# A test-time-training layer with a mixture of experts on one core: experts on rows sorted by group instead of all experts on all rows

## The chip, the cores and the metric

The kernel runs on one core of one Trainium2 chip. The metric is the device time of one execution in microseconds (us). Engines: TensorE (PE, its weight loads PEld), VectorE (DVE), ScalarE (ACT), GpSimd (POOL), and SyncE (SP), which issues DMAs.

## The reference

Input x is 2048 x 256 in f32. After a layer norm over the 256 columns (xn), the output is x + attention part + expert part.

```python
# attention part, heads of 64, chunks of 128 rows, carried state W0, W1, W2, M0, M1, M2
def step(carry, xi):
    ...
    dw0, dw1, dw2 = gradients from q, k, v of this chunk, plus M * mean(momentum)
    M0n, M1n, M2n = dw0, dw1, dw2
    dw0, dw1, dw2 = newtonschulz5 of each        # five iterations X <- aX + (bA + cAA)X, A = X X^T
    return (renorm(W0 + dw0), renorm(W1 + dw1), renorm(W2 + dw2), M0n, M1n, M2n), out
...
scores over a window of 256 keys, softmax, times v
return (ttt_out + attn_out) @ Wo

# expert part: 32 experts in 4 groups of 8, for each row 2 groups and 8 experts in them
scores = sigmoid(xn @ gate_w.T);  top 2 groups by the sum of their 2 best;  top 8 experts in those
xl = xn @ fc1_w.T                                # 256 -> 128
routed = (sum over chosen e of w_e * relu(xl @ w1[e].T)**2 @ w2[e].T) @ fc2_w.T
shared = relu(xn @ shared_up_w.T)**2 @ shared_down_w.T      # 256 -> 512 -> 256
```

Sixteen chunks of 128 rows follow one another, since each needs the weights that the one before leaves. The expert part has no such dependence.

## The kernel before

Everything is f32, and all loops are unrolled. A start prepares chunk 0, then 16 steps follow (`body(i, last)` on each engine), one a chunk. A step i has a head (`k_side`, `q_side`, `grads`, `sums`, `x_first`: key side, query side, gradients and their norm), then 20 stages of Newton-Schulz: in stage st, `ns_turn` (transpose), `ns_gram`, `ns_square` or `ns_apply` by st % 4 on TensorE, for two pairs of heads (g = 0, 1), with `xt` and `ns_x` on ScalarE and `ns_a` and `ns_m` on VectorE in between. The tail has `update`, `row_pow`, `renorm` and `turn_w`/`w_T` (the new weights and their transposes). Semaphores order the engines; each engine runs its own list in order. A dictionary `fill` says by hand what else an engine does after which stage: the attention of step i, the preparation of chunk i+1, and the experts.

Experts: all 32 are computed on all 128 rows of a chunk, in 8 units of 4 experts. `h_up` multiplies the latent rows `xlT` by four weight tiles into the bank HB, `h_relu` on ScalarE does relu and square into `hq`, `y_down` multiplies back into the bank YB, and `y_acc` on VectorE adds YB, scaled by the row's weight (zero where the expert isn't chosen), to `acc`. `y_first` does that for unit 0 on ScalarE. All expert weights (4 MB) stay in SBUF. `route(m)` on VectorE picks groups and experts for one chunk in 13 short instructions or so, one after each half stage. `shared_up` and `out_down` are the shared expert, whose square runs on GpSimd; `fc1` and `out_fc2` change the width. GpSimd does the powers (`power`), `window` and `prep_kl`. SP loads x twice a chunk and stores the result.

```python
fill = {0: [lambda: ln_norm(m), lambda: att_scale(i)], 2: [lambda: y_acc(i, 1)],
...
for st in range(4 * NI):
    for g in range(G):
        if st % 4 in (1, 2):
            (ns_a, ns_m)[st % 4 - 1](i, g, st // 4)
        if st > 10 and routing:
            routing.pop(0)()
    for f in fill.get(st, []):
        f()
```

## Time and profile before

| | |
|---|---|
| median of 3 runs | 794.46 us (792.43 to 794.57) |
| profiled execution | 793.87 us |
| its span in the trace | 792.1 us |
| busy: TensorE, its weight loads | 745.1 us (94%), 639.6 us (81%) |
| busy: VectorE, ScalarE, GpSimd | 612.0 (77%), 463.0 (58%), 184.5 (23%) |
| DMA read, written | 11.41 MB, 2.10 MB |

The profile gives each engine's busy time; a busy TensorE is not one at its peak. The chain that ended last follows the end of the program back from instruction to instruction through whatever released each. The granted clock (PEclk) is 1.00 at full speed and 0.50 at the lower of TensorE's two levels.

### The profile page before, as it was taken

How to read it: one execution, taken by the hardware profiler on the slowest of the kernel's cores; microseconds unless marked ns; L12 is line 12 of the kernel's file. 1: busy time of each engine (PE TensorE's matmuls, PEld its weight loads, DVE VectorE, ACT ScalarE, POOL GpSimd, SP SyncE). 2: the span in 40 equal slices, each digit the busy share in tenths (PEclk: the TensorE clock that was granted, in tenths of full speed). 3: DMA queues.
4: the chain of work that ended last, by engine and by line, in shares of the span. 5: the costliest groups of instructions: out<-in, count | busy, mean ns of one | idle time of the engine just before them, and what ended most of it. 6: DMA issues, size and time to landing. Idle time of an engine off the chain costs nothing.

```text
span 792.1 us, 24469 instructions
## 1 busy us (share of the span) xinstructions
PE 745.1 (94%) x9776; PEld 639.6 (81%) x9776; DVE 612.0 (77%) x2448; ACT 463.0 (58%) x1146; POOL 184.5 (23%) x257
## 2 busy tenths in 40 slices
PE   4899999999999999999999999999999999999997
PEld 2878788788887878878788787887878888788886
DVE  4768778787887868878688786987869878697765
ACT  2665565655655656555556655566555665655754
POOL 1412223122231222312222122220222203222020
PEclk9899999999999999999999999999999999999999
DMA  8100000000000000000000000000000000000000
GB/s 319 68 8 15 9 3 21 2 14 10 2 22 2 16 8 2 22 2 15 8 3 21 2 15 10 2 22 2 15 8 2 22 2 15 8 2 15 2 15 8
DMA packets 9809, 15.07 MB, mean 19 GB/s; under 512 B 1120, under 2 KB 8928, under 8 KB 9440
## 3 DMA queue, kind: packets, MB, share of 16 engines
q1 hardware_dynamic: 7904, 7.80, 3.3%
q10 hardware_dynamic: 1792, 5.70, 1.8%
q8 instruction: 78, 1.28, 0.7%
q14 instruction: 35, 0.29, 0.1%
HBM read 11.41 MB, written 2.10 MB: 17 GB/s over the span
## 4 chain that ended last, share of the span: by engine, by line
PE 74%; ACT 15%; DVE 6%; issue 4%; DMA 1%; SPq 0%; DVEq 0%
PE M L630 23%; PE CC L630 21%; PE HB L630 14%; PE YB L630 11%; ACT hq L415 6%; DVE acc L1332 3%; ACT L570 2%; ACT XT L415 2%; DVE Am L1144 2%; PE CC L739 1%; DMA rows<-in_rows 1%; ACT sq L415 1%; ACT prT L415 1%; PE CC L701 1%; ACT X L415 1%
## 5 line engine op out<-in xcount | busy, mean ns | idle before, releaser
L630 PE MATMUL YB<-e_s,hq 128*128 128x128 f32 x1024 | 140.8, 280 | 11.1 <-DVE acc L1332 9.4
L1332 DVE SCALAR_TENSOR_TENSOR acc<-YB,cw,acc 128x128 f32<-128x128 f32 x448 | 125.3, 342 | 27.3 <-PE YB L630 27.1
L630 PE MATMUL HB<-xlT,e_s 128*128 128x128 f32 x1024 | 143.1, 283 | 0.4 <-ACT xlT L415 0.4
L300 POOL TENSOR_TENSOR r<-r,half 128x3 f32<-128x3 f32 (+1 forms) x78 | 77.9, 1011 | 267.8 <-DVE r L1021 152.6
L630 PEld LDWEIGHTS YB<-e_s,hq 128*128 128x128 f32 x1024 | 124.2, 191 | 17.4 <-issue 15.3
L415 ACT ACTIVATE hq<-HB 128x512 f32<-128x512 f32 x128 | 76.3, 596 | 101.5 <-PE HB L630 101.5
L630 PEld LDWEIGHTS HB<-xlT,e_s 128*128 128x128 f32 x1024 | 126.8, 193 | 6.8 <-ACT xlT L415 0.7
L415 ACT ACTIVATE hq<-hq 128x512 f32<-128x512 f32 x128 | 80.7, 630 | 4.1
L630 PEld LDWEIGHTS CC<-XT 64*64 64x64 f32 x1800 | 43.2, 133 | 32.7 <-ACT XT L415 30.7
L630 PE MATMUL CC<-XT 64*64 64x64 f32 x1800 | 55.6, 232 | 10.3 <-ACT XT L415 10.3
L415 ACT ACTIVATE XT<-CC 128x256 f32<-128x256 f32 x150 | 48.8, 376 | 26.3 <-PE CC L701 26.2
L1144 DVE TENSOR_TENSOR Am<-CC,shifts 128x192 f32<-128x192 f32 x150 | 48.5, 348 | 20.2 <-PE CC L630 20.2
L630 PE MATMUL M<-wall,xnT 128*128 128x512 f32 (+1 forms) x128 | 57.1, 553 | 4.5 <-DMA rows<-in_rows 4.5
L630 PEld LDWEIGHTS CC<-Am 64*64 64x64 f32 x1800 | 42.5, 133 | 22.4 <-DVE Am L1144 16.9
L630 PEld LDWEIGHTS CC<-X,Mp 64*64 64x64 f32 x1800 | 45.5, 133 | 16.5 <-issue 8.8
L630 PE MATMUL CC<-Am 64*64 64x64 f32 x1800 | 54.9, 230 | 3.5 <-DVE Am L1144 3.5
L630 PE MATMUL CC<-X,Mp 64*64 64x64 f32 x1800 | 56.1, 229 | 0.2
L1150 DVE SCALAR_TENSOR_TENSOR Mp<-CC,rests 128x192 f32<-128x192 f32 x150 | 48.6, 350 | 4.8 <-PE CC L630 4.3
L415 ACT ACTIVATE sig<-M 128x512 f32<-128x512 f32 (+1 forms) x32 | 15.7, 490 | 52.2 <-PE M L630 52.2
L415 ACT ACTIVATE X<-CC 128x192 f32<-128x192 f32 x150 | 43.4, 336 | 4.0
L1021 DVE TENSOR_REDUCE r<-sq 128x8 f32<-128x512 f32 x16 | 11.0, 686 | 44.4 <-ACT sq L415 44.4
L331 POOL COPY akT<-akT 128x256 f32<-128x256 f32 x16 | 6.3, 397 | 157.8 <-issue 157.8
(181 smaller groups left out, 1487.3 us busy)
## 6 DMA issues: line engine op xcount, KB each, us to landing
xa<-in_x SPq DMA_DIRECT2D x16, 128.0 KB, 2.2
e_s<-in_e1T ACTq DMA_DIRECT2D x1, 2048.0 KB, 12.7
e_s<-in_e2T ACTq DMA_DIRECT2D x1, 2048.0 KB, 19.2
xr<-in_x SPq DMA_DIRECT2D x16, 128.0 KB, 2.2
out<-ot SPq DMA_DIRECT2D x16, 128.0 KB, 1.7
wall<-in_wall SPq DMA_DIRECT2D x1, 820.0 KB, 5.9
up_s<-in_upT ACTq DMA_DIRECT2D x1, 512.0 KB, 14.3
down_s<-in_downT ACTq DMA_DIRECT2D x1, 512.0 KB, 20.3
```

What stands on the lines that cost most here:

```text
L300: return pool.tensor_tensor(dst, src, expo[:, 0:n], ALU.pow)
L331: pool.tensor_copy(akT[:, :, 0, :], akT[:, :, 1, :])
L415: return nc.scalar.activation(out_, in_, func, **kw)
L570: act.preload_act_table_set("sigmoid_and_others")
L630: return pe.matmul(out_, lhsT, rhs, start=start, stop=stop)
L701: pe.transpose(CA[g][:, P:2 * P], X[g][:, 1:3, :].rearrange("p w c -> p (w c)"), ident[:, :])\
L739: ins = pe.transpose(CA[g][0:HD, w * P:(w + 1) * P], Wn[g][:, w, :], ident[:, :])
L1021: nc.vector.tensor_reduce(r8[:, 0, :], heads(sq8[:, :], 8), AX_X, ALU.add).then_inc(e_ss8, 1)
L1144: nc.vector.tensor_tensor(Am[g][:, :, :], PROD[g], shifts[:, it, :].unsqueeze(1).to_broadcast([P, 3, HD]), ALU.add)\
L1150: nc.vector.scalar_tensor_tensor(Mp[g][:, :, :], PROD[g], NS[it][2], rests[:, it, :].unsqueeze(1).to_broadcast([P, 3, HD]), ALU.mult, ALU. ...
L1332: ins = nc.vector.scalar_tensor_tensor(acc[:, e, :], y, w, acc[:, e, :], ALU.mult, ALU.add)
```

## The change

Four things change together.

1. **Experts on sorted rows.** Layer norm, gate and fc1 of all 16 chunks are computed in step 0 and at the start of step 1 (`ln_turn`, `gate_pair`), and `route()` runs once for all rows, on VectorE from stage 1 of step 1 into step 2. Each row is written twice, once for each of its two groups, with the 8 weights of that group, to its place in a table in HBM sorted by group (32 indirect DMAs of 128 rows by GpSimd, `scatter`). The table has at most 35 tiles of 128 rows, each with one group. A tile needs only its group's 8 experts, in 2 units of 4. SP fetches for each tile the two weight blocks by a register read from `owner_i`, the rows, and the rows' weights, which it writes to HBM and reads back to all partitions (rings of 3 buffers). `h_weight` on VectorE multiplies a unit's 128x512 squares by those weights, and `y_slot` adds all 8 experts of a tile up in PSUM. The tile's result goes to HBM (`keep`); 32 indirect DMAs (`gather`) bring it back in steps 14 and 15, and `last_sum`, `last_turn`, `last_fc2` and `last_out` finish pairs of chunks.
2. **Units in slots.** Each step but the last has 7 slots (`PER`) for a unit's up half and 7 for a down half, two slots later. Row units fill slots 25 to 94 (`FIRST`, 70 units). The shared expert of each chunk is a unit of its own in the slots of `SHARED`, outside these (steps 1 to 3, 13 and 14): 8 matmuls up, 4 of 256 columns down.
3. **Weights group by group.** `update(i, g)` follows stage 19 of each head pair at once with its row sums, and `renorm` scales all three matrices by one multiply.
4. x stays in SBUF, the layer norm is applied by ScalarE, and `prep_qk` moves from stages 4 and 5 to the head, where `shared_up` was.

```diff
+PER = 7
+FIRST = 3 * PER + 4
+SHARED = [PER + 3, PER + 4, PER + 5, PER + 6, 2 * PER, 2 * PER + 1, 2 * PER + 3, 2 * PER + 4, 2 * PER + 6, 3 * PER, 3 * PER + 1,
+          13 * PER + 5, 13 * PER + 6, 14 * PER, 14 * PER + 1, 14 * PER + 2]
...
+            def load(j):
+                b = j % RING
+                if j >= RING:
+                    sp.wait_ge(e_y, at_slot[FIRST + HALVES * (j - RING + 1) - 1][0] + 1)
...
+                first = sp.value_load(owner_i[0:1, j:j + 1], min_val=0, max_val=E - EPG)
+                sp.dma_start(e1_s[b][:, :, :], e1T[:, bass.ds(first, EPG), :]).then_inc(e_tile[b], 16)
+                sp.dma_start(e2_s[b][:, :, :], e2T[:, bass.ds(first, EPG), :]).then_inc(e_tile[b], 16)
...
+            def spread(j):
+                b, n = j % RING, j // RING
+                sp.wait_ge(e_rows[b], 16 * (n + 1))
+                sp.dma_start(cw_d[j, :].rearrange("(p e) -> p e", p=P), xs[b][:, P:ROW]).then_inc(e_gate[b], 16)
+                sp.wait_ge(e_gate[b], 32 * n + 16)
+                sp.dma_start(cwb[b][:, :], cw_d[j, :].partition_broadcast(P)).then_inc(e_gate[b], 16)
...
+            for j in range(RING, NJ):
+                keep(j - RING)
+                load(j)
+                gather_rows(j)
+                spread(j)
...
                 for st in range(4 * NI):
                     for f in fill.get(st, []):
                         f()
+                    for n in range(2):
+                        if (2, 4) <= (i, st) and len(moved) > 2 * NT or GATHER_AT <= (i, st) and moved:
+                            moved.pop(0)()
                 for g in range(G):
                     row_pow(m, g)
...
+            def h_weight(i, k):
...
+                gate = cwb[b][:, :].rearrange("p (t e) -> p e t", e=EPG)[:, c:c + EU, :]
+                nc.vector.tensor_tensor(hb[u % RING][:, :, :], hb[u % RING][:, :, :], gate, ALU.mult).then_inc(e_hw, 1)
...
+                        if st == 4 * NI - 1:
+                            update(i, g)
+                        if routing and (i, st) >= (SORT_STEP, 1):
                             routing.pop(0)()
```

TensorE in a middle step (step 7), from `q_out` behind stage 2 to the squares of stage 6; `e_s` are expert weights, `hq` and `hb` a unit's squares. Before:

```order
L630 MATMUL M<-WT,gh 128x128 x2
L637 MATMUL M<-ident,xn 128x128 x2
L630 MATMUL CC<-X,Mp 64x64 x12
L630 MATMUL YB<-e_s,hq 128x128 x4
L700 MATMUL CC<-ident,X 64x128
L701 MATMUL CC<-ident,X 128x128
L700 MATMUL CC<-ident,X 64x128
L701 MATMUL CC<-ident,X 128x128
L630 MATMUL M<-wall,xnT 128x512
L630 MATMUL CC<-XT 64x64 x12
L630 MATMUL M<-wall,xnT 128x512
L630 MATMUL CC<-Am 64x64 x12
```

The same place now:

```order
L808 MATMUL M<-WT,gh 128x128 x2
L808 MATMUL CC<-X,Mp 64x64 x12
L808 MATMUL HB<-xsT,e_s 128x128 x4
L901 MATMUL CC<-ident,X 64x128
L902 MATMUL CC<-ident,X 128x128
L901 MATMUL CC<-ident,X 64x128
L902 MATMUL CC<-ident,X 128x128
L808 MATMUL M<-wall,xnT_all 128x276 x2
L808 MATMUL CC<-XT 64x64 x12
L808 MATMUL YB<-e_s,hb 128x128 x4
L808 MATMUL CC<-Am 64x64 x12
```

The transposes of xn and the two wide products for q and k are gone from here, the product for v stands two stages earlier, and a unit's half takes the place behind stage 5.

VectorE in step 1, stages 1 to 3, now (`Am` and `Mp` are the handoffs of Newton-Schulz, one for each head pair; MAX on `cwb` is the routing of all 16 tiles, in a buffer that the tiles' weights use later):

```order
L1390 TENSOR_TENSOR Am<-CC,shifts 128x192
L1508 TENSOR_TENSOR cwb<-sc,rows 128x512
L1390 TENSOR_TENSOR Am<-CC,shifts 128x192
L1514 MAX cwb<-cwb 128x8 x16
L1396 SCALAR_TENSOR_TENSOR Mp<-CC,rests 128x192
L1514 MAX cwb<-cwb 128x8 x16
L1396 SCALAR_TENSOR_TENSOR Mp<-CC,rests 128x192
L1514 MAX cwb<-cwb 128x8 x32
```

Before, nothing of the routing stood ahead of stage 11. Now 16 maxima stand between the two head pairs' `Mp`.

GpSimd in step 2, from the power for the query side on, now:

```order
L421 TENSOR_TENSOR r<-r,neghalf 128x4
L436 DMA sorted_rows<-xsrc,dest_i 4480x136 x10
L421 TENSOR_TENSOR r<-r,half 128x8
L436 DMA sorted_rows<-xsrc,dest_i 4480x136 x14
L470 COPY akT<-akT 128x2x128
L471 COPY vw<-vw 128x256
L473 COPY vw<-raw 128x256
L436 DMA sorted_rows<-xsrc,dest_i 4480x136 x2
L462 TENSOR_TENSOR kl<-qkn,lr 128x256 x2
L462 TENSOR_TENSOR vl<-sl,lr 128x256
L436 DMA sorted_rows<-xsrc,dest_i 4480x136 x6
L421 TENSOR_TENSOR r<-r,half 128x3 x2
```

The 32 indirect DMAs stand ahead of or between `prep_n8` (128x8), `window`, `prep_kl` and `row_pow` (128x3); before, these followed one another with nothing between.

## Rows read from the trace of the kernel before

**Rows 1.** The page: span, and busy time of each engine

```profile
span 792.1 us, 24469 instructions
...
PE 745.1 (94%) x9776; PEld 639.6 (81%) x9776; DVE 612.0 (77%) x2448; ACT 463.0 (58%) x1146; POOL 184.5 (23%) x257
```

**Rows 2.** The page: the chain that ended last, by engine

```profile
PE 74%; ACT 15%; DVE 6%; issue 4%; DMA 1%; SPq 0%; DVEq 0%
```

**Rows 3.** The chain in order of time, head of step 7 (start, us, what)

```profile
370.50 1.65 PE CC L630 x8
...
379.88 0.61 ACT hq L415
```

**Rows 4.** The same chain, steps 7 and 8: wide products, tail, head of step 8

```profile
387.44 0.86 PE M L630 x2
...
388.92 1.06 PE M L630 x2
...
413.23 2.37 PE M L630 x12
415.60 0.89 PE HB L630 x8
...
419.52 1.65 PE CC L630 x8
...
426.97 1.00 PE M L630 x8
...
428.87 0.02 issue
```

**Rows 5.** The same chain, step 7, scores to the gram product of stage 17

```profile
400.17 1.06 PE M L630 x4
...
407.85 1.28 ACT L570
...
409.58 0.73 PE CC L630 x24
```

**Rows 6.** The page's costliest groups: second products of experts, their sums

```profile
L630 PE MATMUL YB<-e_s,hq 128*128 128x128 f32 x1024 | 140.8, 280 | 11.1 <-DVE acc L1332 9.4
L1332 DVE SCALAR_TENSOR_TENSOR acc<-YB,cw,acc 128x128 f32<-128x128 f32 x448 | 125.3, 342 | 27.3 <-PE YB L630 27.1
```

**Rows 7.** VectorE: groups by shape, timeline, and the instructions on xn (min/median/max)

```profile
L1031 DVE TENSOR_TENSOR qkn<-sl,r 128x512 f32<-128x512 f32 x16 | 11.1, 691 | 0.6
...
400.43 0.37 DVE L1272 MAX8 g<-sbias 128x8 f32<-128x8 f32 x4
...
L1002 DVE TENSOR_SCALAR xn<-xa,mv,rstd x16: 410/1129/1132, 4.9 to 723.8; 128x256 f32<-128x256 f32 x16
```

**Rows 8.** Busy time by window: a piece of the start, and step 7

```profile
core 0: us, PE busy (x) PEld busy (x) DVE busy (x) ACT busy (x) POOL busy (x), PEclk, DMA share, GB/s
...
20.00:22.00 2.00, 0.89 (x4) 0.92 (x4) 1.42 (x14) 1.11 (x4) 1.67 (x2) 0.50 0.95 347
...
367.00:416.00 49.00, 47.17 (x640) 40.61 (x639) 38.49 (x154) 29.21 (x73) 11.27 (x16) 1.00 0.03 10
```

**Rows 9.** GpSimd: groups by shape

```profile
L300 POOL TENSOR_TENSOR r<-r,half 128x3 f32<-128x3 f32 x62 | 51.7, 850 | 115.2 <-DVE r L1117 71.3 <-DVE r L1160 43.9
L300 POOL TENSOR_TENSOR r<-r,half 128x8 f32<-128x8 f32 x16 | 26.2, 1636 | 152.6 <-DVE r L1021 152.6
L365 POOL TENSOR_TENSOR us<-ur 128x512 f32<-128x512 f32 x16 | 19.2, 1202 | 9.5 <-ACT ur L415 9.5
```

**Rows 10.** Timeline (first product of step 0, of step 15, an issue) and DMA issues

```profile
27.07 0.60 PE L630 MATMUL CC<-WT,qkT 128*128 128x256 f32 x2
...
763.81 1.13 PE L630 MATMUL M<-qkT,WT 128*128 128x128 f32 x8 [0.95 <-ACT WT L415]
...
763.41 0.43 SPq L285 DMA_DIRECT2D xr<-in_x  x1
...
xa<-in_x SPq DMA_DIRECT2D x16, 128.0 KB, 2.2
```

More of the change, by code:

```diff
@@ L30 @@
 F32 = mybir.dt.float32
+I32 = mybir.dt.int32
+U32 = mybir.dt.uint32
 AX_X = mybir.AxisListType.X
@@ L393, in _ @@
             prep_n8(0)
-            window(0, True)
+            for n in range(1, 5):
+                prep_rstd(n)
+            window(0)
             prep_kl(0)
@@ L1410, in _ @@
             prep_silu_v(0)
[L1411 to L1418 removed]
+            prep_ss8(0)
+            lr_a(0)
+            prep_mean(0)
+            ln_stats(1)
+            ln_stats(2)
+            prep_qkn(0)
+            lr_b(0)
+            ln_shift(1)
+            ln_shift(2)
+            ln_stats(3)
+            ln_stats(4)
+            lr_c(0)
+            ln_shift(3)
+            ln_shift(4)
+            routing = route()
             dve.wait_ge(e_later, 16 * NLATER)
+            nc.vector.tensor_scalar(before[:, :], fixed[:, 2, :], 0.0, None, ALU.is_lt)
+            dve.wait_ge(e_jrow, 1)
+            nc.vector.tensor_copy(jrow_f[:, :], jrow[:, :])
+            nc.vector.tensor_scalar(jrow_p[:, :], jrow[:, 0:NT], float(P), None, ALU.mult).then_inc(e_jrow, 1)
             body(0, False)
```

1044 lines of the change are left out of this document (666 added, 378 removed).

## Prediction

> **What bounds it now.** I read the page first. The profiled execution took 793.9 us, 792.1 of them span, with TensorE busy 94% and VectorE 77% [rows 1]. The chain that ended last runs 74% through TensorE, 15% through ScalarE, 6% through VectorE [rows 2]: mostly the matmul stream binds, and the rest is handoffs. From there I went to the chain in order of time for one step in the middle, then to groups by line and to the timeline at both ends. One step begins with its `k_side` at 370.50 and the next at 419.52 [rows 3, 4], so a step is 49.0 us; from 27.07 in step 0 to 763.81, where step 15 starts with `q_side` [rows 10], it is 49.1 a step. Step 15 takes 28.3 us more to the end. Inside a step I separate three parts. The head (419.52 to 428.87, 9.35 us) is an unbroken row of TensorE work. The five Newton-Schulz iterations, 20 stages, run from 379.88 to 413.23, 33.4 us. The tail, 413.23 to 419.52, is 6.3 us of TensorE work without a gap [rows 3, 4]. Eight 128x128 matmul instructions, one expert unit up or down, cost 0.89 us where nothing waits [rows 4].
>
> **The normal step afterwards (steps 3 to 13, eleven of them).** Only two of four groups serve a row, so 35 tiles of 8 experts give 70 units instead of 128, spread 7 to a step. Head: the two halves of `shared_up` (0.89 and 1.00) give way to `prep_qk` and `prep_qk_more`, two 128x512 instructions each. In step 7 such a half cost 0.86 to 1.06 [rows 4]: no gain. Stages: 11 unit halves stood there, 7 stand there now, 4 x 0.89 = 3.6 less; `prep_qk` and `prep_turn` leave too, 1.9 + 0.2; two transposes of sorted rows come, 0.2. That is 5.5 us less TensorE work. But three halves stood between `att_scores` and the gram product of stage 17, 400.17 to 409.58 [rows 5], and one stands there now. There the chain is mask, maximum, exponentials, a unit's relu and square, X, prT, the 1.28 us table load and XT, none of which the change shortens: the 1.8 us taken out there are filler, replaced by waiting. So 3.7 us remain. Stages 7, 10, 14, 17 and 19 now have no filler at all and show the handoff of VectorE or ScalarE; I charge 0.6. On the other side the four `acc` instructions of a unit (342 ns each, 448 in all, with 9.4 us of TensorE waiting for them [rows 6]) become one 128x512 multiply, about 0.69 by the same shape [rows 7]; I credit 1.0. Tail: TensorE has y, h, `out_wo`, y, h = 4.4 us instead of 5.8, but the relu and square of the last unit now stand ahead of `w_T` on ScalarE. 4.4 + 0.15 + 0.60 + 0.63 + 0.7 for the first two WT copies is 6.5: +0.2. Step = 49.1 - 3.7 + 0.6 - 1.0 + 0.2 = **45.2**, or 11 x 3.9 = 43 us saved. Both ends: 43.6 if the fixed part hides behind nothing, 47 if bare handoffs cost 0.4 each.
>
> **Weights.** Updating group by group starts a group's square and sum some 0.5 us earlier, and one multiply replaces three. The tail is held by ScalarE (above), which hides it: nothing; 0.5 a step if that cover is gone.
>
> **Step 0.** Its units are absent; seven pairs of layer-norm transposes (0.44) and six gate pairs (eight instructions of 160 columns, my estimate 1.1 between 0.11 and 0.31 each) stand there. 44: -5.
>
> **Step 1 carries the routing of all 16 tiles on VectorE.** Stages 1 to 9 get 64 MAX8 (0.37 for four [rows 7], 5.9), 16 MAX8 of 32 columns and 16 match-and-replace (my estimates, 0.12 and 0.25 each, between the 0.09 of a small MAX8 and the 0.69 of 512 columns: 5.9), three 512-wide operations (2.1), 2 us of small ones: 16 us. They stand between `ns_a` or `ns_m` of group 0 and of group 1, so every stage waits for them. VectorE was 79% busy in a step [rows 8]; without `acc` and per-tile routing about half of those 16 us fits into its gaps. +8: 53, or +3.9 against before. TensorE gets four double-size ups and two downs late in it, the same sum as normal.
>
> **Step 2 is the worst.** Five shared ups (1.78) and six shared downs (1.73) make 19.3 us where a normal step has 12.5; 1.3 of the difference falls into waits, +5.5. Five 512-wide routing operations in stages 0 to 3: +3. And 32 indirect DMAs go out on GpSimd from stage 4 on, two a stage. The trace has none. The bounds: below, 0.45 us, a queue's plain DMA issue [rows 10]; above, 1.64, GpSimd's slowest instruction; between them 0.85 and 1.2 [rows 9]. I take 1.1, nearest to the middle rows. Then GpSimd needs 35.2 + 4.8 (n8, the window copies, `prep_kl`) = 40 us until `row_pow`; TensorE's stages reach that point about 28.5 us after stage 4: 29.3 us of stages in a normal step (33.4 - 3.7 + 0.6 - 1.0), less 5.7 for the first four, plus 2.6 for three doubled halves, plus some 2 for `update` and row sums. Another 2 us or so of waiting disappears behind the longer tail. Behind the scatters are queued `prep_n8` (for `prep_qkn`), `prep_kl` (for `grads`) and `row_pow` (for `renorm`, `turn_w`): **+10**. Step 2 = 64, +15.
>
> A rule of the Trainium skill, SBUF — State Buffer, section SBUF: two separate sides, speaks against this change: VectorE and GpSimd exclude each other on a shared port for a whole instruction. This trace agrees: xn beside GpSimd's square takes 1129 ns, alone 410 [rows 7]. If descriptor writing holds the port likewise, some 12 such operations late by 0.7 in each of two steps add 17 us. The skill's DMA: Bandwidth & Descriptors, section Latency and other measured facts, puts the start of a GpSimd DMA at about 1 us; by it the sum would be 6 us lower.
>
> **Step 14** has the 32 gathers from stage 0 on: 35.2 + 6 against 33: +7 after slack; 1.4 more shared work; two of the last pairs (transpose, fc2) 2. 55.6: +6.5. **Step 15** has no units; what remains is q_side, scores, probabilities, `out_wo`, and two pairs after it, its length I take from before: 28.3, less 14 unit halves, two `shared_up` and two `out_down` parts (12.5 + 1.8 + 1.8 = 16.1), plus six pairs of last sums (two transposes and two 128x256 products, 1.1 each, 6.5), plus 2.3 for VectorE and ScalarE work in the attention chain that units covered: 21. -7.3. **Start**: no fc1, no two units before `k_side`: -1.
>
> **Sum**: -43 - 5 + 4 + 15 + 6.5 - 7.3 - 1 = -31, 793.9 - 31 = **763 us**. The median before, 794.5, lies 0.6 above the profiled one; changes under 0.3% (2.4 us) can't be told from none.
>
> **Expert weights and rows** are fetched anew for each tile, hidden in my sum. Per tile SP orders a store, a register load, two 512 KB loads, rows, and the gate weights twice, the last broadcast to 512 KB. At the 347 GB/s of the start [rows 8] 1 MB is 3.0; a small one takes 2.2 from issue to landing [rows 10]. Rows are there after 6.5 us (three issues of 0.43, 3.0 for the loads, 2.2 for the rows behind them), the broadcast after 14 (0.5 + 2.2 for the gate weights' way out, 0.5 + 1.5 + 2.2 for the way back, and some 0.6 for the register load). The nearest needs are two and a bit over three slots later: with the freeing y at the tail's start, 8.4 us for the transposed rows and 18 for the multiply. Covered by 2 and by 4 us.
>
> **Rivals.**
> - *Cheap issue, TensorE binds more.* Indirect DMAs at 0.6: both waits vanish (-17), and steps of 44.2 (-11): 735. For it: TensorE at 94%. Against: the fixed chain of [rows 5]. 0.22.
> - *GpSimd becomes the bound (the slower side).* Each us more per indirect DMA costs 32 x 2 = 64 us, in steps 2 and 14. 763 + 64(c - 1.1) passes 794 at c = 1.6, the slowest present instruction; at 2.0 it is 820. For it: 128 separate rows in one instruction. Against: GpSimd idles 77% [rows 1]. 0.16.
> - *The tile ring is late.* 17 of 35 tiles start near the tail; 1.5 us late each: +26, 789. For it: four DMAs wait one for another. 0.12.
> - *The port, or the clock.* With the port lock 780. While TensorE waits some 10 us in steps 2 and 14 its clock may go to its low level: in the trace it was at 0.50 from 20 to 22 us [rows 8], after the waits of the start. A head of 9.35 at half speed is +9 each, 781. 0.10.
> - *My forecast*, 750 to 775: 0.40.
>
> **Range.** Loaded steps 43.6 to 47 give -18 to +20, issue cost 0.6 to 1.6 -17 to +32. 733 to 797 leaves out the dear GpSimd case and the very best. Faster: my case, the cheap one and most of the ring and port cases, 0.79; same 0.05; slower 0.16.
>
> **What would show it.** Right: `k_side` to `k_side` near 45 in steps 4 to 12; no `acc`; TensorE about 80% busy; long first-half stages in step 1 ended by VectorE; in steps 2 and 14 GpSimd busy without gap, and `renorm` waiting for it; few waits for DMA at xs or cwb. Wrong if an indirect DMA costs far from 1.1 us, if waits for tile DMAs appear in every step, or if normal steps come out near 41 (I overrated the handoffs) or 48.

## Result: slower, 829.3 us, and the profile after

The changed kernel takes 829.26 us (median of 4 runs, 827.45 to 831.44) against 794.06 (4 runs, 792.43 to 794.57) before: ratio 1.044, 95% interval 1.043 to 1.046. The forecast was 763 and faster. The profiled execution took 829.26 us, 827.5 of them span. Of the runs below, one of `e19_memset_again` took 905.9 us at a granted clock of 0.73; it is in the slow state and is left out of that kernel's median.

The page of the changed kernel: span, busy time, the granted clock in 40 slices, and the chain that ended last by engine.

```profile
span 827.5 us, 22394 instructions
...
PE 681.7 (82%) x8887; PEld 560.4 (68%) x8887; DVE 542.7 (66%) x1893; ACT 410.7 (50%) x1061; POOL 228.4 (28%) x299
...
PEclk9799789987999999999999999999999999999768
...
PE 49%; DVE 19%; ACT 15%; issue 9%; POOL 7%; DMA 1%; SPq 0%; ACTq 0%; POOLq 0%; DVEq 0%
```

Beside [rows 1, 2]: TensorE has 63 us less work, as meant, but it carries 49% of the chain instead of 74%. VectorE went from 6 to 19%, GpSimd from nothing to 7%. Apart from the start, where the kernel before had a smaller one, three dips stand in the clock's row: step 1, step 2, and step 14 with the end.

Busy time by window, cut from one `q_side` to the next: step 0, step 1, step 2, steps 6 and 5, step 14, the last stretch, and the 7 us after step 2's renorm.

```profile
core 0: us, PE busy (x) PEld busy (x) DVE busy (x) ACT busy (x) POOL busy (x), PEclk, DMA share, GB/s
27.48:74.17 46.69, 39.61 (x555) 32.10 (x555) 32.77 (x123) 31.80 (x89) 15.30 (x23) 0.98 0.01 2
74.17:132.68 58.51, 49.05 (x578) 39.50 (x577) 43.70 (x260) 24.82 (x65) 9.79 (x14) 0.85 0.15 56
132.68:208.40 75.72, 53.82 (x606) 43.29 (x605) 34.57 (x117) 23.97 (x60) 41.71 (x47) 0.86 0.11 35
351.14:398.46 47.32, 41.37 (x594) 34.66 (x593) 34.20 (x107) 27.13 (x72) 10.25 (x14) 1.00 0.44 132
302.40:351.14 48.74, 42.87 (x594) 36.01 (x593) 34.29 (x107) 26.68 (x70) 10.25 (x14) 0.96 0.38 122
733.69:801.26 67.57, 47.68 (x571) 37.78 (x569) 30.77 (x109) 21.45 (x56) 40.68 (x46) 0.85 0.13 37
801.26:827.50 26.24, 18.62 (x74) 14.35 (x74) 12.93 (x31) 6.44 (x16) 1.01 (x1) 0.81 0.20 71
202.00:209.00 7.00, 4.95 (x17) 3.68 (x18) 3.98 (x17) 2.20 (x8) 2.21 (x4) 0.50 0.29 84
```

Each stretch against the forecast (steps 3 to 13 run from 208.40 to 733.69):

| stretch | forecast | measured | off by |
|---|---|---|---|
| step 0 | 44 | 46.7 | +2.7 |
| step 1 | 53 | 58.5 | +5.5 |
| step 2 | 64 | 75.7 | +11.7 |
| steps 3 to 13, each | 45.2 | 47.75 | +2.55, 28 in all |
| step 14 | 55.6 | 67.6 | +12.0 |
| last stretch | 21 | 26.2 | +5.2 |

The sum is 65 us, practically the whole distance of 66 from 763 to the profiled execution. So every row of the forecast was too low; steps 3 to 13 (28 us) and steps 2 and 14 (24 us) carry most of it.

GpSimd in step 2, and who waits for it (timelines of POOL, DVE and PE; start, us, what, idle time before and its releaser):

```profile
155.68 1.01 POOL L421 TENSOR_TENSOR r<-r,neghalf 128x4 f32<-128x4 f32 x1 [13.86 <-DVE r L1447]
156.89 1.22 POOL L436 DMA_INDIRECT sorted_rows<-xsrc,dest_i  x1 [0.20 <-issue]
...
168.53 0.96 POOL L436 DMA_INDIRECT sorted_rows<-xsrc,dest_i  x1 [0.30 <-issue]
169.51 1.68 POOL L421 TENSOR_TENSOR r<-r,half 128x8 f32<-128x8 f32 x1
...
201.09 0.96 POOL L436 DMA_INDIRECT sorted_rows<-xsrc,dest_i  x1 [0.30 <-issue]
202.08 1.71 POOL L421 TENSOR_TENSOR r<-r,half 128x3 f32<-128x3 f32 x2
...
171.23 0.17 DVE L1271 TENSOR_SCALAR r<-r 128x8 f32<-128x8 f32 x1 [5.81 <-POOL r L421]
...
203.00 0.17 DVE L1416 TENSOR_SCALAR r<-r 128x3 f32<-128x3 f32 x1 [15.20 <-POOL r L421]
...
204.02 1.73 PE L940 MATMUL CC<-ident,Wn 128*64 128x128 f32 x6 [12.38 <-DVE Wn L1422]
```

An indirect transfer is 0.96 us of GpSimd and 0.30 until the next, 1.26 from start to start. The transfers start behind the power for the query side (128x4), for whose input GpSimd waited 13.9 us. VectorE waits 5.8 us for n8 (the power of `prep_n8`) and 15.2 us for the row power; TensorE idles 12.4 us, and when it resumes, its granted clock is at 0.50, the lower of its two levels.

The gate multiply of an expert unit in the changed kernel, by shape, and the head of step 6 from its first `k_side` product to the first transpose of stage 0 (chain in order of time):

```profile
L1680 DVE TENSOR_TENSOR hb<-hb,cwb 128x512 f32<-128x512 f32 x70 | 76.1, 1087 | 6.0 <-ACT hb L554 5.6
```

```profile
349.73 0.91 PE CC L808 x4
...
353.99 1.01 DVE hb L1680
...
358.13 1.00 DVE hb L1680
...
359.46 0.37 DVE X L1373
...
359.88 0.30 PE CC L901
```

It takes 1087 ns, not the 691 ns of the plain 128x512 multiply in [rows 7]: its second operand is read at every eighth element. Two of these multiplies are pieces of the chain in the head, and between the two products shown the chain runs mostly through VectorE; before, the head was a row of TensorE work alone [rows 4].

### The profile page after: what moved, and what is told of

Read it like the earlier page. It is cut to its first block, busy times and chain, and to the rows that moved or that the text cites. A ratio compares the mean times of both kernels' runs of the same rounds, so it can differ in the third digit from the quotient of the medians.

```text
span 827.5 us, 22394 instructions
## 1 busy us (share of the span) xinstructions
PE 681.7 (82%) x8887; PEld 560.4 (68%) x8887; DVE 542.7 (66%) x1893; ACT 410.7 (50%) x1061; POOL 228.4 (28%) x299
## 4 chain that ended last, share of the span: by engine, by line
PE 49%; DVE 19%; ACT 15%; issue 9%; POOL 7%; DMA 1%; SPq 0%; ACTq 0%; POOLq 0%; DVEq 0%
PE CC L808 15%; PE YB L808 11%; PE HB L808 8%; PE M L808 8%; ACT hb L554 5%; POOL sorted_rows L436 3%; DVE Am L1390 2%; ACT L742 2%; DVE hb L1680 2%; ACT XT L554 2%; PE CC L901 1%; POOL xsrc L446 1%; ACT pr L554 1%; POOL r L421 1%; DVE r L1485 1%
## 5 line engine op out<-in xcount | busy, mean ns | idle before, releaser
L554 ACT ACTIVATE hb<-HB 128x512 f32<-128x512 f32 x86 | 51.0, 593 | 106.0 <-PE HB L808 106.0
L1680 DVE TENSOR_TENSOR hb<-hb,cwb 128x512 f32<-128x512 f32 x70 | 76.1, 1087 | 6.0 <-ACT hb L554 5.6
L808 PE MATMUL YB<-e_s,hb 128*128 128x128 f32 x560 | 79.9, 287 | 0.0
L808 PE MATMUL HB<-xsT,e_s 128*128 128x128 f32 x560 | 78.0, 282 | 0.0
L808 PEld LDWEIGHTS YB<-e_s,hb 128*128 128x128 f32 x560 | 72.4, 198 | 7.5 <-issue 4.8
L808 PEld LDWEIGHTS HB<-xsT,e_s 128*128 128x128 f32 x560 | 67.9, 191 | 2.7
L808 PEld LDWEIGHTS CC<-XT 64*64 64x64 f32 x1800 | 45.2, 135 | 31.9 <-ACT XT L554 24.9
L808 PEld LDWEIGHTS CC<-Am 64*64 64x64 f32 x1800 | 45.3, 137 | 22.7 <-DVE Am L1390 16.1
L901 PE MATMUL CC<-ident,X 128*64 128x128 f32 x150 | 40.4, 289 | 22.3 <-ACT X L554 20.6
L808 PE MATMUL M<-wall,xnT_all 128*128 128x512 f32 (+1 forms) x128 | 55.4, 541 | 2.7 <-DMA rows<-in_rows 2.0
L554 ACT ACTIVATE hb<-hb 128x512 f32<-128x512 f32 x86 | 54.2, 630 | 2.7
L901 PEld LDWEIGHTS CC<-ident,X 128*64 128x64 f32 x150 | 17.0, 113 | 33.4 <-ACT X L554 26.2
```

Source lines behind the costliest of these rows:

```text
L554: return nc.scalar.activation(out_, in_, func, **kw)
L808: return pe.matmul(out_, lhsT, rhs, start=start, stop=stop)
L901: pe.transpose(CA[g][0:HD, 0:P], X[g][:, 0, :], ident[:, :])
L1680: nc.vector.tensor_tensor(hb[u % RING][:, :, :], hb[u % RING][:, :, :], gate, ALU.mult).then_inc(e_hw, 1)
```

## Experiments

All times are medians; the kernel before, run beside them, took 794.0 to 794.7 us in every group. The experiments ran on four chips, here A to D, and it turned out that this matters, so each group names its chip. For the changed kernel's first measurement, with which most runs below are compared, the chip isn't recorded. Steps are again cut from `q_side` to `q_side`.

### Chip A: no transfers, paced transfers, gate view, no MAX8

`e1_no_moves`, 796.1 us (ratio 1.005, interval 1.003 to 1.007):

```diff
-                    sp.wait_ge(e_scat, 16 * 2 * NT)
+                    sp.wait_ge(e_rt, RT_ALL)
...
-            moved = [lambda n=n: scatter(n) ...] + [lambda n=n: gather(n) ...]
+            moved = []
```

> Left out: all 64 indirect transfers of rows, so the expert tiles compute on zero rows and the output is not the reference's; everything else is issued as in the changed kernel. Theory (GpSimd's queue): the powers and the products kl wait behind transfers that take 1.26 us each, so without them step 2 falls from 75.7 to about 58 us, step 14 from 67.6 to about 50, the slow clock after them goes, and the time is 829 - 18 - 17 = about 794 (790 to 800). Rival (TensorE's and VectorE's added work, the shared units and the rest of the routing, makes step 2 long; the last gathers make step 14 long only by being waited for at the end): step 2 stays above 68, and the time stays above 812.

```profile
131.26:186.46 55.20, 47.37 (x607) 39.04 (x606) 34.04 (x115) 23.40 (x60) 10.02 (x14) 1.00 0.11 34
711.71:766.37 54.66, 44.42 (x570) 35.27 (x569) 30.62 (x109) 21.33 (x56) 10.12 (x14) 0.97 0.02 7
```

These are the windows of steps 2 and 14 without transfers: 55.2 instead of 75.7 and 54.7 instead of 67.6, and the clock is back at 1.00 and 0.97. The transfers cost 33 us. Without them the change still gains nothing (0.3 to 0.7% slower than before), where the forecast had a gain: the transfers are only half of the miss.

`e2_paced`, 834.4 us:

```diff
+                move({3: 4, 14: 4}.get(i, 0))
...
-                    for n in range(2):
-                        if (2, 4) <= (i, st) and len(moved) > 2 * NT or GATHER_AT <= (i, st) and moved:
-                            moved.pop(0)()
+                    move(int((2, 4) <= (i, st) < (3, 5) or (14, 0) <= (i, st)))
...
+                move({2: 7, 14: 8}.get(i, 0))
```

> Same 64 transfers and the same work, but handed out one per Newton-Schulz stage, and several at once only behind the powers of the rows and behind k_u, where GpSimd is idle anyway; the scatter ends in step 3 instead of step 2. Theory (their place in the queue costs, not their number): n8, kl and the row powers come on time, step 2 takes about 60 us, step 14 about 52, and the time is near 803 (797 to 812). Rival (the transfers cost by what they do while they run, port or memory traffic, or the amount of GpSimd's work): the time moves by less than 6 from 829. A second rival: the late end of the scatter makes the first tile wait in step 3, which then is 5 us or more longer than 47.

Steps 2, 3 and 14 took 67.9, 57.5 and 73.1 us: not the forecast 60 and 52. What step 2 gained, step 3 gave back, and step 14 became longer. This run has 34 us of the late marks described next, so it doesn't tell what pacing alone would do.

`e3_gate_view`, 852.2 us, and `e4_no_max8`, 855.0 us:

```diff
-                gate = cwb[b][:, :].rearrange("p (t e) -> p e t", e=EPG)[:, c:c + EU, :]
+                gate = cwb[b][:, :].rearrange("p (e t) -> p e t", e=EPG)[:, c:c + EU, :]
```

```diff
-                            for n in range(NG):
-                                ins = nc.vector.max(g8[:, t, n, :], sbias[:, t, n * EPG:(n + 1) * EPG])
+                        return nc.vector.tensor_copy(g8[:, t, :, :].rearrange("p t g c -> p t (g c)"), sbias[:, t, :])
```

> Only the view of the gates changes: the multiply in h_weight reads its second operand with neighbouring elements instead of every eighth one, so it multiplies by the gates of other rows and experts, and the output is not the reference's. Theory: the stride makes it 1.08 instead of 0.69 us, and since the multiplies of places 6 and 0 stand in the head of a step on VectorE, ahead of the momentum's sums, an ordinary step falls from 47.8 to about 46.9 and the time by about 10 (6 to 19), to about 819. Rival (the multiply is slow for another reason, its size or a port): it stays above 1.0 us and nothing moves. Second rival (it is hidden): it falls to 0.7 us and the time moves by less than 3.

> The 64 MAX8 that find the best two of each group of experts become 4 copies of the first ones of each group, so other groups are chosen and the output is not the reference's. Theory (VectorE's routing work fills the gaps of step 1 and delays Newton-Schulz there): some 5.5 us of VectorE work less, step 1 falls from 58.5 to about 54 and the time by 4 (3 to 6). Rival (step 1 is long by the shared units on TensorE and its clock): step 1 stays above 57.5 and the time moves by less than 1.5.

The multiply fell to 685 ns (group of VectorE, `e3_gate_view`):

```profile
L1680 DVE TENSOR_TENSOR hb<-hb,cwb 128x512 f32<-128x512 f32 x70 | 48.0, 685 | 9.8 <-ACT hb L554 9.8
```

and an ordinary step from 47.3 to 46.7. So the stride is real and worth 0.6 us in a step at full clock; over the eleven it was 4.4 (520.9 against 525.3), as one more of them had a lowered clock. Without the MAX8 step 1 stayed at 58.7: they alone cost nothing. But both kernels, each with less work, were 23 to 26 us slower than the changed kernel. All of it lies in steps 2 and 14: 87.3 and 87.9 in the one, 85.7 and 87.9 in the other. A mark is the semaphore update by which an engine tells another that an instruction is done. In these steps ACT and DVE show waits for TensorE's marks that end long after the product's end by the profile, 69 and 70 us in sum (waits over 0.5 us of this kind, added up from the timelines; 34 in `e2_paced`). The changed kernel's own trace has none. I call them late marks.

### Chip B: GpSimd free for transfers, head order, plain transfers, written gates

`e5_powers_dve`, 862.8 us. VectorE takes the other work of GpSimd in steps 2 and 14:

```diff
+            def dve_n8(m):
+                if m in ON_DVE:
+                    dve.wait_ge(e_ss8, m + 1)
+                    power(r8[:, 1, :], r8[:, 0, :], half, 8).then_inc(e_n8, 1)
...
+                    if st == 4:
+                        move({2: 26, 14: 21}.get(i, 0))
```

> All 64 indirect transfers stay, but in steps 2 and 14 GpSimd does nothing beside them from stage 4 on: n8, the window copies, kl/vl and the row powers of these two steps go to VectorE, where the powers stand in as a multiply by 0.5, so the output is not the reference's; the last 6 scatters follow in step 3. Theory 1 (the place in GpSimd's queue costs): steps 2 and 14 come near the 55.2 and 54.7 us that they took without the transfers, at most 3 above, and the time is near 802 (796 to 810). Theory 2 (while indirect transfers run, the marks that TensorE sets after its products reach ScalarE and VectorE late, as in the runs with other gates and without the MAX8, where such waits of 1 to 14 us sum to 70 us): steps 2 and 14 stay above 62 each, ACT and DVE show waits without a known releaser beside the transfers, and the time stays above 818.

Theory 1 alone is refuted on this chip: steps 2 and 14 took 88.5 and 84.4 although GpSimd did nothing else beside the transfers, with 90 us of late marks. `e6_head_order`, 861.8 us:

```diff
                 k_side(i)
-                if i:
-                    h_weight(i - 1, 6)
                 q_gate(i)
                 grad(i)
+                if i:
+                    h_weight(i - 1, 6)
```

> VectorE does the gate multiply of place 6 behind the momentum's squares and sums of a step's head instead of ahead of the query's gate; nothing else changes. Theory (on the chain it stands twice in the head, 1.01 us at 353.99 and again at 358.13; the second lies beside GpSimd's powers, the first beside nothing): an ordinary step falls by about 1.0 us, from 47.3 to 46.3, 12 us over the program. Rival (TensorE's last products before it are late anyway): an ordinary step stays at 47.3. The total can move by 20 us either way through steps 2 and 14, as the last runs' did; the steps 3 to 13 decide.

An ordinary step took 47.6 to 47.7, no gain but 0.3 worse. In its head the copy of the sums comes at 6.3 instead of 6.8 us after `q_side`, but then both row powers of GpSimd lie bare on the chain (1.72 us), where before the second multiply had covered them. A piece on the chain is not worth its length. `e8_plain`, 797.4 us:

```diff
-                pool.indirect_dma_start(
-                    xs_d[:, :], bass.IndirectOffsetOnAxis(ap=dest_i[:, t, j:j + 1], axis=0),
-                    xsrc[:, t, j, :], None).then_inc(e_scat, 16)
+                pool.dma_start(xs_d[n * P:(n + 1) * P, :], xsrc[:, t, j, :]).then_inc(e_scat, 16)
```

> The 64 indirect transfers become plain ones of the same bytes, issued by GpSimd in the same places, so the rows are not sorted and the output is not the reference's. If it is the making of the row lists on GpSimd that costs, each takes far less than 1.26 us of GpSimd, and the time goes to that of the run without transfers, 796 (790 to 802). If it is the bytes, or any transfer of GpSimd's queue, it stays at 820 or more.

Its GpSimd timeline in step 2:

```profile
155.44 5.53 POOL L436 DMA_DIRECT2D sorted_rows<-xsrc  x10
162.37 1.66 POOL L421 TENSOR_TENSOR r<-r,half 128x8 f32<-128x8 f32 x1 [1.40 <-DVE r L1263]
```

Ten plain transfers take 5.5 us where ten indirect ones took 12.6, n8 no longer waits for them, and no mark is late. So on chip B neither the bytes nor the queue matter, but the indirect transfer; whether by its instruction or by its scattered rows, this run doesn't separate. `e9_no_moves_head_gate`, 976.2 us:

```diff
-                sp.dma_start(cw_d[j, :].rearrange("(p e) -> p e", p=P), xs[b][:, P:ROW]).then_inc(e_gate[b], 16)
+                sp.dma_start(cw_d[j, :].rearrange("(e p) -> p e", p=P), xs[b][:, P:ROW], allow_slow_non_contiguous=True).then_inc(e_gate[b], 16)
```

> Without the 64 transfers (the tiles compute on zero rows, the output is not the reference's), with the gate multiply of place 6 behind the momentum's sums, and with the gates written expert by expert, so that the multiply reads neighbours at no change of their meaning. Theory (the two head multiplies and their stride are on the chain): against the 796 without transfers an ordinary step falls from 47.3 to about 45.9, 12 to 18 us in all, to about 781. Rival (writing the gates in elements of 4 bytes takes so long that tiles wait for them): waits of VectorE on cwb appear and the steps stay above 47.

Its page, chain by engine and by line:

```profile
DMA 45%; PE 25%; issue 8%; DVE 7%; SPq 7%; ACT 6%; another core or an unknown queue 1%; POOL 0%; ACTq 0%; POOLq 0%; DVEq 0%
```

The rival held: written in elements of 4 bytes, the gates make SP's queue the bound; the next tiles' rows stand behind them, and steps 4 to 13 take 52 to 71 us. This is the failure that the forecast's ring rival spoke of; the change as made doesn't have it. Late marks appear here too (42 us in sum), with no GpSimd transfer in the kernel.

### Chip C: no multiply, filler, old update, more products

`e10_no_gate_multiply`, 791.2 us, on top of e1's edit:

```diff
-                    pe.wait_ge(e_hw, n + 1)
+                    pe.wait_ge(e_hs, 2 * u + 2)
```

> Without the 64 transfers and, on top, without the gate multiply of the expert units (TensorE waits for ScalarE's square alone), so the output is not the reference's. Compared with the run without transfers (796.1 us, ordinary steps 47.3 and 48.7). Theory (the multiply, in the head and between the square and the product, is what keeps an ordinary step above the predicted 45.2): ordinary steps fall to 45.7 or less, the time to about 778. Rival (TensorE's own chain through Newton-Schulz bounds the step, and the multiply is beside it, as moving one of them out of the head gave nothing): ordinary steps stay above 46.6, the time above 787.

One ordinary step's window: 46.2 us, between both theories, 1.1 less than with the multiply. Steps 9 to 12 took 47.7 to 48.0, with the clock down, so that steps 3 to 13 gained 9.6 us in all (515.7 against 525.3). Its window, and the head of that step in its chain:

```profile
286.37:332.55 46.18, 40.64 (x594) 34.68 (x593) 27.29 (x100) 26.63 (x70) 10.02 (x14) 1.00 0.40 129
```

```profile
284.96 1.57 PE CC L809 x8
...
293.26 0.89 PE YB L809 x8
...
294.26 0.11 PE CC L902
```

The head is a row of TensorE work again. Cutting ordinary steps at full clock in three, from the first `k_side` product to the first transpose of stage 0, to the end of the last `ns_apply`, to the next `k_side`, shows where the multiply costs (us):

| | head | 20 stages | tail | step |
|---|---|---|---|---|
| before | 9.2 | 33.5 | 6.3 | 49.0 |
| forecast, cut the same way | 9.2 | 29.4 | 6.5 | 45.1 |
| changed kernel | 10.15 | 30.4 | 6.7 | 47.3 |
| `e3_gate_view` (read without the stride) | 9.6 | 30.4 | 6.7 | 46.7 |
| `e10_no_gate_multiply` | 9.1 | 30.4 | 6.7 | 46.2 |

All of it is in the head. The stages take 30.4 us with the multiply and without.

`e11_filler`, 824.8 us, powers in the place of both kinds of transfer:

```diff
-                pool.indirect_dma_start(
...
+                power(beat[...][:, 6 * n:6 * n + 5 + n % 2], neghalf, half, 5 + n % 2)
```

> Each of the 64 indirect transfers becomes one small power on GpSimd of about the same length (1.2 to 1.3 us from start to start), in the same place; nothing is moved, the tiles compute on zero rows and the output is not the reference's. Theory A (GpSimd's occupied queue alone): steps 2 and 14 take again about 75 and 67 us and the time is that of the changed kernel, 829 (822 to 836). Theory B (what the transfers do outside GpSimd, since in five runs TensorE's marks came late beside them): the powers in the queue cost, but less than half of the 33 us, and no wait without a known releaser appears. The measured split between the two is the difference to 796 on the one side and to 829, and to the 850 to 863 of the runs with late marks, on the other.

```profile
133.43:208.83 75.40, 55.61 (x607) 45.01 (x605) 34.40 (x116) 23.88 (x60) 49.15 (x47) 0.86 0.08 25
732.78:800.75 67.97, 50.78 (x570) 40.10 (x569) 30.67 (x109) 21.45 (x56) 48.61 (x46) 0.81 0.02 5
```

Its windows of steps 2 and 14 are those of the changed kernel, 75.4 and 68.0 against 75.7 and 67.6, although nothing is moved. That is the decisive run for the changed kernel: what costs there is GpSimd's occupied queue ahead of n8, kl (the products of `prep_kl`) and the row powers. On the same chip the changed kernel's two steps are 76.9 and 70.0 (`e18_again` below), 1.5 and 2.0 more; in step 2 1.1 of that is the filler's shorter queue (row powers 69.5 us after `q_side`, there 70.6), and at most the rest can belong to what the transfers do elsewhere.

`e12_old_update`, 800.2 us, with e1's edit, the update for both groups together and the old three multiplies:

```diff
-                        if st == 4 * NI - 1:
-                            update(i, g)
...
+                update(i)
```

> Without the 64 transfers, and with the update of the weights as before the change, both groups together (output not the reference's, as the tiles compute on zero rows). The prediction counted the group by group update at nothing. Theory: ordinary steps stay within 0.3 us of 47.3 and 48.7 and the time within 4 us of 796. Rival (it shortens the tail): the time rises by 6 us or more, 0.5 per step.

Steps 3 to 13 sum to 525.6 us, against 525.3 in e1: no difference. The 4 us of the total lie in the other steps and at the ends, which also scatter between the runs without transfers: step 1 58.4 to 59.9, step 2 55.2 to 59.8, the last stretch 22.7 to 27.6.

`e13_more_products`, 800.9 us, with e1's edit:

```diff
+                if i == 1 and k <= 2:
+                    pe.wait_ge(e_xnT, NL)
+                    shared_up(k)
```

> Without the 64 transfers, and with three further sets of 16 shared products (up of tiles 0 to 2, their result unused) in the empty slots 7, 8 and 9 of step 1; the output is not the reference's. Theory (step 1 is long because TensorE has too little to do there, so the granted clock falls to 0.5 to 0.8 in 83 to 107 us, and not by VectorE's routing, as leaving out the 64 MAX8 left step 1 at 58.7): the clock of step 1 rises from 0.85 to above 0.93 and the step falls from 58.4 to 55 or less although it has 6 us more of products. Rival (the routing on VectorE, which is 95% busy in 83 to 98 us): the step stays at 58 or rises.

Step 1 rose from 58.4 to 63.8 with the clock at 0.87. The products did not bring the clock back, so this run doesn't tell what the clock costs. `e8_plain` does, by chance: its step 1 is the same program and had the clock at 0.94 (window below). It took 56.6 us, where the three others on chip B, with the same step 1 too, took 58.6 to 59.2 at 0.85 or 0.86. So some 2 us of step 1 are the clock.

```profile
73.22:129.84 56.62, 45.48 (x578) 37.17 (x577) 43.75 (x260) 24.52 (x65) 9.79 (x14) 0.94 0.16 58
```

### Chip D: no routing, 32 rows, one memset, pairs behind

`e14_no_routing`, 786.9 us, with e1's edit:

```diff
-                        step().then_inc(e_rt, 1)
+                        nc.vector.memset(owner[:, len(rest) % NJ:len(rest) % NJ + 1], 0.0).then_inc(e_rt, 1)
```

> Without the 64 transfers, and with the 45 routing steps on VectorE cut down to one small memset each (the same marks, no scores used), so the output is not the reference's. Theory (the whole of the routing, its 45 steps in a row behind each other, is what step 1 has over an ordinary step; the 64 MAX8 were only a part beside other waits): step 1 falls from 58.4 to about 50 and the time by 6 to 10 us from 796. Rival (step 1 is long by what TensorE does there with its clock down: the shared units, the prefix products and too little else): step 1 stays at 56 or more.

Step 1 without routing, beside step 1 of e1 (two kernels' windows):

```profile
74.48:123.74 49.26, 42.67 (x579) 35.42 (x578) 29.19 (x144) 24.46 (x65) 10.03 (x14) 0.97 0.18 66
```

```profile
72.85:131.26 58.41, 48.87 (x578) 39.41 (x577) 43.73 (x260) 24.82 (x65) 9.79 (x14) 0.85 0.15 56
```

The routing as a whole costs 9.1 us there: 14.5 us of VectorE's time, in steps that wait one for another, of which the MAX8 are the part that was hidden. The clock went from 0.85 to 0.97 with it, so the 9.1 hold some 2 us of clock too (`e8_plain` above).

`e15_rows32`, 862.7 us, and `e16_one_memset`, 856.6 us:

```diff
-                    xs_d[:, :], bass.IndirectOffsetOnAxis(ap=dest_i[:, t, j:j + 1], axis=0),
-                    xsrc[:, t, j, :], None).then_inc(e_scat, 16)
+                    xs_d[:, :], bass.IndirectOffsetOnAxis(ap=dest_i[0:32, t, j:j + 1], axis=0),
+                    xsrc[0:32, t, j, :], None).then_inc(e_scat, 16)
```

```diff
-            nc.vector.memset(ones[:, :], 1.0)
+            nc.vector.memset(ones[:, 0:HD], 1.0)
+            nc.vector.memset(ones[:, HD:P], 1.0)
```

> All 64 indirect transfers stay, but each moves the rows of the first 32 partitions alone, so most rows stay zero and the output is not the reference's. If GpSimd's time goes with the rows, each takes about 0.3 to 0.5 us, steps 2 and 14 fall below 62 and the time to about 805. If it is a price per instruction, the spacing stays near 1.26 us and steps 2 and 14 near 75 and 67, the time near 829. If waits without a known releaser appear (as in the runs of 850 to 863 us) with a quarter of the rows too, they come with the instruction, not with the bytes.

> The changed kernel with one memset of the start split into two halves: one instruction of VectorE more, nothing else. If the late marks depend on where the transfers happen to fall against TensorE's work, this too can bring them: then steps 2 and 14 take 80 to 88 us each and the time is 850 or more. If the changed kernel's 829 is stable and the slower runs came from their edits, it stays at 829 (825 to 833) with steps of 75.7 and 67.6.

A transfer of 32 rows still takes 0.87 us of GpSimd, 1.17 from start to start (`e15_rows32`), so the price is almost all the instruction's; the other 96 rows add 0.09:

```profile
163.40 0.87 POOL L436 DMA_INDIRECT sorted_rows<-xsrc,dest_i  x1 [0.30 <-issue]
```

Both have the late marks, 87 and 73 us of them, steps 2 and 14 at 84.6 to 90.4. This is how they look in `e16_one_memset`: timelines of PE and DVE, with one of POOL's transfers beside them.

```profile
176.25 0.69 PE L808 MATMUL CC<-XT 64*64 64x64 f32 x24
...
181.02 0.36 DVE L1391 TENSOR_TENSOR Am<-CC,shifts 128x192 f32<-128x192 f32 x1 [5.07 <-remote]
...
181.44 0.34 PE L808 MATMUL CC<-Am 64*64 64x64 f32 x6 [1.47 <-issue]
182.47 0.40 PE L808 MATMUL CC<-Am 64*64 64x64 f32 x3 [0.69 <-issue]
...
183.22 0.26 PE L808 MATMUL CC<-Am 64*64 64x64 f32 x1 [0.36 <-issue]
...
184.62 0.38 PE L808 MATMUL CC<-Am 64*64 64x64 f32 x2 [1.14 <-issue]
...
186.42 0.95 POOL L436 DMA_INDIRECT sorted_rows<-xsrc,dest_i  x1 [0.30 <-issue]
186.78 0.36 DVE L1391 TENSOR_TENSOR Am<-CC,shifts 128x192 f32<-128x192 f32 x1 [5.40 <-remote]
```

The 24 products for which the two `Am` wait end at 176.94 by the profile, but VectorE starts them at 181.02 and 186.78, 4.1 and 9.8 us later. Twelve small products that wait for the first `Am` alone leave TensorE in groups of 6, 3, 1 and 2 over 3.6 us. VectorE's own operations keep their length (0.36). The ends of products are modelled, so whether the products or their marks are late isn't shown.

`e17_pairs_behind`, 800.2 us, with e1's edit:

```diff
-                if i == LAST - 1:
-                    last_turn(0)
-                    last_fc2(0)
...
                 turn_w(m, 0)
                 turn_w(m, 1)
+                if i == LAST - 1:
+                    last_turn(0)
+                    last_fc2(0)
...
```

> Without the 64 transfers (output not the reference's), and with the first two pairs of the last layer, which stood ahead of the turning of the new weights at the end of step 14 on TensorE, ScalarE and VectorE, moved behind it. Theory (the weights of step 15 waited for those two pairs, each a round of VectorE, TensorE, ScalarE, TensorE): step 14 falls from 54.7 to about 51, the last stretch grows by less, the time falls by 2 to 4 us from 796. Rival (the pairs only change place): the sum of step 14 and the last stretch, 77.4, stays within 1 us.

Step 14 and the last stretch together took 80.9 us, against 77.4 in e1 and 79.1 to 83.6 in e10, e12, e13 and e14: no gain is to be seen, the theory fell. The pairs still stand ahead of step 15's first products, so step 14, cut at `q_side`, could not become shorter by their whole length (it took 56.9).

### Chip C again: does the program decide, or the chip?

`e18_again`, 826.2 us, is the changed kernel unchanged; `e19_memset_again`, 827.3 us, is e16's kernel.

> The changed kernel itself, unchanged, once more, on the same chip as the next run. If the late marks belong to the program (its instructions' places and their times against each other), it takes 829 again (826 to 833), steps 75.7 and 67.6, with no wait without a known releaser. If they belong to the chip on which it ran, it takes 850 or more here.

> The kernel with the split memset (856.6 us) once more, beside the changed kernel on one chip. If the program decides, it takes 850 to 863 while the changed kernel takes 829. If the chip decides, both take the same within 5 us.

Windows of steps 2 and 14 of `e19_memset_again`, then of steps 2, 14 and the last stretch of `e18_again`:

```profile
133.69:210.56 76.87, 57.23 (x606) 46.12 (x605) 34.68 (x117) 24.12 (x60) 41.35 (x47) 0.83 0.11 35
733.03:802.77 69.74, 49.30 (x570) 39.06 (x569) 30.83 (x109) 21.51 (x56) 41.18 (x46) 0.85 0.13 35
```

```profile
134.12:211.05 76.93, 55.79 (x606) 45.22 (x605) 34.67 (x117) 23.92 (x60) 41.37 (x47) 0.85 0.10 34
733.54:803.54 70.00, 49.22 (x571) 39.00 (x569) 30.69 (x109) 21.45 (x56) 41.50 (x46) 0.85 0.13 35
803.54:826.20 22.66, 13.96 (x74) 10.17 (x74) 12.85 (x31) 6.45 (x16) 1.01 (x1) 1.00 0.24 82
```

The same program that took 856.6 us on chip D takes 827.3 on chip C, beside the changed kernel's 826.2, with no late mark. Alone, `e18_again` fits the first branch of its expectation; the run beside it decides: where it runs matters, not the program. Each chip was seen with indirect transfers in one round only, so the chip and the round on it can't be told apart. The transfers' own packets don't differ: 1.7% of the span of the 16 DMA engines on D, 1.8% on C. That the excess of e3 to e6 came from where they ran and not from their edits is inferred from this pair, since the changed kernel itself was not run on A or B; `e2_paced`, with half the late marks on chip A, says that the edit has a share there. Totals compare only within a chip. On chip C itself the filler's 824.8 and the changed kernel's 826.2 agree. No variant with its output intact was faster than the kernel before; the best ones, 786.9 and 791.2, leave out the moving of rows and more.

## Why the prediction was wrong

1. **The gate multiply, the largest error.** The step that failed: "become one 128x512 multiply, about 0.69 by the same shape; I credit 1.0". It takes 1.09 us by the stride of its operand, and it is no relief: without any multiply an ordinary step is 46.2, with it 47.25. The forecast's sum without that credit is 49.1 - 3.7 + 0.6 + 0.2 = 46.2. So instead of -1.0 the term was +1.05, 2.05 a step, 22.5 us in eleven (20.6 if the clock that falls without it is counted, as in e10). The table under `e10_no_gate_multiply` says where. The credit was taken in the stages, and they took 30.4 us instead of 29.4, with the multiply or without: if the other terms hold, the leaving of `acc` brought nothing there. The price fell due in the head, which the forecast took for a row of TensorE work with "no gain" and no loss. It is mostly VectorE's chain now, and two of the multiplies stand in it: 1.0 us, of which 0.6 goes with the stride (`e3_gate_view`). I had looked up the shape and neither the access pattern nor the place. Why leaving out `acc` brought nothing was not tried. That head, stages and tail come out at 9.1, 30.4 and 6.7 without the multiply, where the forecast without its credit has 9.2, 30.4 and 6.5, bears out the rest of the sum part by part, though not each term.
2. **Clock dips in ordinary steps.** Not forecast at all. Four of the eleven are 1.3 to 1.5 us longer with the clock at 0.96 or 0.97 (the window 302.40:351.14 is one), 5.8 us in all. The kernel before was at 1.00 in these steps. TensorE is busy 42.9 us in that window, 41.4 in its neighbour 351.14:398.46 at 1.00, and 47 of 49 in [rows 8]. That the missing filler brings the dips is likely but not shown: the same step stands with a dip and without.
3. **Steps 2 and 14.** "I take 1.1" for an indirect transfer: 1.26 measured, which is 5 us in each of the two steps. The mechanism, powers waiting behind the transfers, was right, and `e11_filler` shows it to be nearly all there is in the changed kernel. But +10 and +7 were 20.5 and 12.9, taken against e1 (its steps 2 and 14 are at the low end of the runs without transfers, 55.2 to 59.8 and 54.5 to 57.4). The timelines of GpSimd give the rest. In e1 the row powers of step 2 start 46.6 us after `q_side`, in the changed kernel 69.4 us, 22.8 later; in step 14 it is 45.7 and 58.6, 12.9 later.

```profile
177.91 0.89 POOL L422 TENSOR_TENSOR r<-r,half 128x3 f32<-128x3 f32 x1 [2.14 <-DVE r L1405]
```

In step 2 the forecast let the transfers start with stage 4. TensorE was there at 152.5, but GpSimd's list has the query side's power ahead of them, whose input came at 155.68, so the first one started at 156.89. That is 4.4 us more of delay, with 5.1 from the price and 1.7 from stages that were shorter than the 28.5 of the forecast (26.8 in e1), 11 us in all. In step 14 the same power, in the middle of the gathers, kept GpSimd idle for 3.6 us. The clock at 0.50 after TensorE's long wait adds a little more: the 8 `k_side` products that begin the next step's head took 2.86 us there, 1.65 in [rows 4]. The clock rival and the GpSimd rival were written as alternatives to the forecast, but one brings the other.

4. **Step 14's base.** Without gathers it is 54.7, where the forecast had 48.6. "Two of the last pairs (transpose, fc2) 2" was the term: in e1 they take from 758.4 to 764.3, 5.9 us, since each is a round over four engines. Moving them behind the turning of the weights did not help (`e17_pairs_behind`), so only the size of the term is shown, not a cure. The other 2 us of the 6 are open.
5. **Step 1.** "+8 for routing" came near: 9.1 measured, but some 2 of them are the lowered clock, which the term didn't have. What failed is the base beneath it, 49.3 without routing where 45 was taken.
6. **Weights group by group at nothing**: right (`e12_old_update`, 0.3 us over eleven steps).
7. **The last stretch** (26.2 for 21) goes with the clock: the same program took 22.7 us there at 1.00 in `e18_again`, where this execution had 0.81, and the runs without transfers go from 22.8 us at 1.00 (e1) to 27.6 at 0.74 (e12). So 3.5 of the 5.2 us are clock. **Step 0** (46.7 for 44) was too low as well; what makes it was not tried.
8. **Rivals.** Cheap issue: refuted by 1.26. GpSimd the bound: its own formula, 763 + 64(c - 1.1), gives 773 at 1.26, 10 us of the 16 by which the two waits passed the forecast's 17. Ring late: not in this change; `e9` shows what it looks like. Port lock: not seen, VectorE's additions beside transfers take their usual 0.36, and 0.69 for `qkn`; no gate multiply ran beside a transfer. The Trainium skill, SBUF — State Buffer, section SBUF: two separate sides, on which that rival rested, also says that TensorE never waits for the DMA side. On chips A, B and D TensorE ran in drips beside the indirect transfers. Whether it waited for SBUF there or for something else no run shows, so the page is neither borne out nor refuted.

Of the signs, GpSimd busy without gap and renorm waiting for it came true, TensorE at 82% too; `k_side` to `k_side` near 48 was named as a sign of being wrong, and it came (47.75). Two slips in the working change little: 49.1 a step counts from a `k_side` product to a `q_side` one, like with like it is 49.0; and 28.5 is 28.2 by its own terms.

**Open**: why three of four chips let TensorE's products and marks come late beside indirect transfers (and beside writes of 4 bytes), and chip C does not. Not tried: the changed kernel itself on A, B or D, or one chip in several rounds.

## What to carry to other kernels

Before crediting an operation that replaces several, find a row with its shape and its stride, and then find its places on the chain: 128x512 read at every eighth element took 1.09 us instead of 0.69, and of seven in a step only the two in the head cost anything. Before letting transfers start at some stage, look at what the same engine's list has in front of them. Transfers that an engine issues are work of that engine: in front of small operations on the chain they cost what exceeds the engine's free time (here 45 us of queue before the row powers cost 20.5), and an operation of the same length does the same, which a filler in their place tests cheaply. And where TensorE is left with idle stretches, count its lower clock as part of the wait's price.

## What the hardware showed that I had not expected

- An indirect transfer costs 1.26 us of GpSimd for 128 rows and 1.17 for 32; a plain one 0.55 (5.53 for ten).
- The same program took 856.6 us on one chip and 827.3 on another, while the kernel before took 794.0 and 794.7 on them. All of the difference lies beside the indirect transfers, 73 us of late marks against none.
- Gates written in 4-byte elements, 35 writes of 4 KB, brought the time from 796 to 976 us, with two edits of VectorE's work beside them (`e9_no_moves_head_gate`).
